# A longer clear between gathers, and every group transposed by itself, in a pairwise-interaction kernel

## The reference

```
e = stack([tbl_f[ids[:, f]] for f in range(32)], axis=1)     # 1024 x 32 x 64
p, q = e[:, ROW], e[:, COL]                                  # the 496 pairs of fields
kp = einsum('bpj,ipj->bpi', p, kernel)                       # kernel 64 x 496 x 64
z = sum(kp * q, axis=-1)                                     # 1024 x 496
h = concatenate([z, dense_ctx], axis=1)                      # 1024 x 512
h = relu(h @ W_top1 + b_top1);  h = relu(h @ W_top2 + b_top2);  y = h @ W_top3
```

## Time and profile before

| | |
|---|---|
| median of 3 runs | 626.92 us (626.18 to 627.76) |
| profiled execution | 622.16 us, span of its instructions 620.2 us |
| granted TensorE clock, mean | 0.884 |
| TensorE busy | 502.4 us (81%) |
| VectorE busy | 305.6 us (49%) |
| GpSimd busy | 273.9 us (44%) |
| ScalarE busy | 67.4 us (11%) |
| DMA, mean | 38 GB/s |

### The profile page before, as it was taken

How to read it: one execution, slowest core, us unless ns; L and a number is a source line. 1 busy time by engine, 2 the same in 40 slices (tenths; PEclk the granted TensorE clock), 3 DMA queues, 4 the chain that set the end, 5 groups by cost and what they waited for, 6 DMA issues and landing times.

```text
span 620.2 us, 10322 instructions
## 1 busy us (share of the span) xinstructions
PE 502.4 (81%) x4290; PEld 309.4 (50%) x4290; DVE 305.6 (49%) x324; ACT 67.4 (11%) x130; POOL 273.9 (44%) x492
## 2 busy tenths in 40 slices
PE   1764444589999786678898768699889999999998
PEld 0432200356666454446565435466566666766443
DVE  3611200166776364337455436467377788787000
ACT  0001000011111021011001001011001211100112
POOL 5888887555557676352727445555700000000000
PEclk9975655599999998798978879899989999999999
DMA  5521212033331111010101011010100030000000
GB/s 154 179 71 23 58 23 61 18 90 90 104 109 43 31 24 26 13 25 9 22 16 23 15 23 28 17 22 17 22 12 1 14 110 10 2 10 2 0 0 0
DMA packets 15318, 23.56 MB, mean 38 GB/s; under 512 B 5506, under 2 KB 7810, under 8 KB 15145
## 3 DMA queue, kind: packets, MB, share of 16 engines
q1 hardware_dynamic: 6884, 14.14, 7.8%
q0 software_dynamic: 7808, 8.01, 6.5%
q10 hardware_dynamic: 580, 0.76, 0.4%
HBM read 20.79 MB, written 0.00 MB: 34 GB/s over the span
## 4 chain that ended last, share of the span: by engine, by line
PE 67%; another core or an unknown queue 13%; issue 10%; DVE 7%; DMA 2%; ACT 0%; SPq 0%; DVEq 0%
PE kp L539 37%; PE z_ps L556 19%; DVE prod L485 6%; PE kp L577 4%; PE tr_ps L523 3%; PE kp L583 2%; PE tr_ps L515 2%; DMA k_sb<-in_tbl 2%; DVE prod L495 1%; PE kp L590 0%; ACT pair L397 0%; ACT prod L441 0%; DVEq L484 0%; SPq L334 0%
## 5 line engine op out<-in xcount | busy, mean ns | idle before, releaser
L485 DVE TENSOR_TENSOR prod<-kp,pair 128x1024 f32<-128x1024 f32 x224 | 261.4, 1218 | 239.0 <-PE kp L539 137.7
L539 PE MATMUL kp<-pair,k_sb 64*128 64x256 f32 x1984 | 286.7, 420 | 63.8 <-issue 32.4
L377 POOL DMA_INDIRECT raw<-in_tbl,ids_sb x244 | 232.8, 954 | 174.8 <-PE tr_ps L523 99.9
L539 PEld LDWEIGHTS kp<-pair,k_sb 64*128 64x128 f32 x1984 | 202.8, 203 | 138.8 <-issue 69.5
L556 PE MATMUL z_ps<-prod,ones_sel 128*32 128x256 f32 x1984 | 141.5, 389 | 24.2 <-issue 22.5
L556 PEld LDWEIGHTS z_ps<-prod,ones_sel 128*32 128x32 f32 x1984 | 65.0, 111 | 94.5 <-issue 57.3
L397 ACT ACTIVATE pair<-tr_ps 128x512 f32<-128x512 f32 (+1 forms) x40 | 20.5, 512 | 351.5 <-PE tr_ps L523 249.4
L381 POOL MEMSET rest<- 128x64 f32 x244 | 40.9, 168 | 0.4
L495 DVE TENSOR_TENSOR prod<-kp,pair 128x512 f32<-128x512 f32 x48 | 30.2, 683 | 8.9 <-issue 6.6
L523 PE MATMUL tr_ps<-ident,raw 128*128 128x128 f32 x122 | 23.8, 309 | 11.4 <-issue 10.8
L515 PE MATMUL tr_ps<-prod,k_sb 125*64 125x256 f32 x96 | 16.6, 521 | 15.7 <-DMA k_sb<-in_tbl 13.4
(11 more groups left out here) (10 smaller groups left out, 9.0 us busy)
## 6 DMA issues: line engine op xcount, KB each, us to landing
k_sb<-in_kd SPq DMA_DIRECT2D x15, 512.0 KB, 3.7
raw<-in_tbl,ids_sb POOLq DMA_INDIRECT x244
pair<-pair SPq DMA_DIRECT2D x32, 64.0 KB
k_sb<-in_tbl SPq DMA_DIRECT2D x6, 250.0 KB
k_sb<-in_w SPq DMA_DIRECT2D x1, 1024.0 KB, 5.0
hot_ids_sb<-in_hot_ids SPq DMA_DIRECT2D x3, 250.0 KB
z_sb<-in_dense ACTq DMA_DIRECT2D x1, 512.0 KB
k_sb<-in_w SPq DMA_DIRECT2D x1, 512.0 KB, 5.7
```

Source lines behind the costliest of these rows:

```text
L377: nc.gpsimd.indirect_dma_start(raw[:, r % RAW_RING, i, n, :], None, tables[f], bass.IndirectOffsetOnAxis(ap=ids_sb[:, 2 * b + i, f:f + 1], ...
L485: nc.vector.tensor_tensor(prod[:, u % PROD_RING, :, :].rearrange("p q (i n) -> p (q i) n", i=UNIT_SLOTS), kp[u % KP_RING][:, :, :].rearran ...
L539: last = nc.tensor.matmul(kp[u % KP_RING][:, q, i * WIDTH:(i + 1) * WIDTH], k_sb[rows, x, :], pair[rows, group_place(st, owner // 2), :], ...
```

## The change

Two constants and the list of places. The clear behind each gather covers 192 columns, not 64 (the scratch tile grows with it). In stages 1 to 3 an event is one group, as in stage 0, so there are 64 events, and the list says where each stands.

```
-REST = 64
+REST = 192

-STAGES = (1, 2, 2, 2)
+STAGES = (1, 1, 1, 1)

-TRANSPOSE_AT = [0, 0, 0, 1, 2, 4, 7, 10, 13, 17, 23, 25, 31, 36, 41, 47, 52, 57, 64, 69, 75, 85, 93, 98, 109, 114,
-                123, 128, 137, 144, 155, 160, 171, 176, 185, 190, 199, 206, 217, 222]
+TRANSPOSE_AT = [0, 0, 0, 1, 2, 4, 7, 10, 13, 17, 23, 25, 31, 36, 41, 47, 52, 57, 61, 63, 64, 66, 69, 72, 75, 79, 85,
+                87, 93, 98, 103, 109, 114, 119, 123, 125, 126, 128, 131, 134, 137, 141, 147, 149, 155, 160, 165,
+                171, 176, 181, 185, 187, 188, 190, 193, 196, 199, 203, 209, 211, 217, 222, 227, 233]
```

## The result

The changed kernel takes 560.19 us (559.72 to 560.39, four runs) against 627.34 for the kernel before beside it: a ratio of 0.8914 (0.8864 to 0.8964), 10.9% faster. The forecast was 24%. The time lies in the range with rivals 1 and 3 (450 to 600 us), not in the forecast's own (455 to 510 us), and the size of the gain does not fit.

A forecast was written before the change was run, and what follows sets the result against it. TensorE sets the pace, but gathers 1.39 us apart delay its signals. Unit 2 at 39.6, 371.5 for 246 units and a 50.4 tail give 461.5 us; with overhead 467, plus 10 makes 477 us, own range 455 to 510.

The forecast's parts named there:

- Rival 1: Only short runs help, spacing does not: the first 80 gathers still hold TensorE back, 550 to 600 us; chance 0.22.
- Rival 3: Cure in part: a load of 1.43 in each 1.53 us delays each signal 1.4 us; 510 to 540 us; chance 0.08.
- a service that each gather needs and that takes about 1.43 us: In runs of gathers 1.39 us apart, this unnamed need builds up a backlog, and TensorE's signals stand behind it.
- My own test: TensorE at half speed before 120 us, lumps 1.5 us apart: no service of 1.43 us exists, rival 1 or 2 holds.
- rival 2: A continuous GpSimd hurts at whatever spacing, and the longer clear is paid on each gather: 661 us, slower; chance 0.16.
- The two rows that "fitted": First eleven gather intervals average 1.45 us, signal at once; recovery took about 4 us after 80 gathers, 1.1 after eight.
- The sum: Whole kernel with signals in time: span 461.5 us, 467 us as median of runs, plus 10 us for imperfections: 477 us.
- 246 units x 1.51 = 371.5 us: TensorE's stretch from unit 2 to the last unit's products, at 1.51 us a unit with signals in time.
- The clear: Behind each gather on GpSimd: 0.14 us more, a gather each 1.53 us, 34 us more in all.
- GpSimd's supply: Gathers end at 378 us, beside TensorE with some 0 to 10 us of slack, costing nothing or a few us.
- The single transposes: In stages 1 to 3 GpSimd is released for four gathers, not eight; ScalarE's 4 us more is hidden.
- the complete cure: Signals in time throughout the kernel: likeliest time 477 us, chance 0.50.

The follow-up runs named there:

- e7: Kernel before, with GpSimd clears in place of all gathers but the first four, clear of 64 columns kept: 448.78 us, ratio 0.7106.
- e14: Kernel before, with a plain copy of the table's first 128 rows in place of each gather, clear of 64 columns kept: 450.24 us, ratio 0.7395.
- e12: Changed kernel with a clear of 288 columns in place of 192, a gather each 1.575 us: 480.96 us, ratio 0.7624.
- e3: Changed kernel with a clear of 320 columns in place of 192, a gather each 1.60 us: 482.21 us, ratio 0.7677.
- e5: Changed kernel with a clear of 256 columns in place of 192, a gather each 1.55 us: 523.82 us, ratio 0.8272.
- e15: Changed kernel with a clear of 448 columns in place of 192, a gather each 1.71 us: 507.67 us, ratio 0.8338.

## Why the prediction was wrong in size

**The step that failed** is "a service that each gather needs and that takes about 1.43 us". From it followed that any spacing over 1.44 us would leave nothing late. At 1.49 us 85 us were late, at 1.55 us 71, and only from 1.575 to 1.60 us did it all but end (37 and 11). I had taken the distance of TensorE's lumps for the time of a service. They follow the gathers: 1.39 gave 1.43 and 1.46, 1.49 gave 1.50. My own test for that stood in the prediction, and it went against me; but the rivals 1 or 2 that were to hold in that case do not hold either. The two rows that "fitted" carried less than I put on them. The first eleven intervals of 1.45 us end at 20.83 us, and TensorE's first products start at 24.6 us. Of the two recoveries only the one of 4 us was worked out (80 x 0.04 = 3.2 us); the same sum gives 8 x 0.04 = 0.3 us for the other, and 1.1 us were measured.

**The sum was right once its condition held.** It gave 477 us with the signals in time throughout; the kernels for which that nearly holds took 481 and 482 us. That it is so near is luck in part: in e7 and e14, where nothing is late, the 246 units take 362 us, 1.47 us each for the 1.51 of the sum, and the whole 449 and 450 us. What e12 and e3 take over that is the signals that are still late and the waits for gathers. The terms in the changed kernel: unit 2 starts at 35.3 us (33 to 39.6 was said), the tail is 50.4 us, as said. The term that failed is 246 units x 1.51 = 371.5 us; it took 507.5 - 35.3 = 472 us, 101 more. Late signals come to 85 us, 5 of them at unit 0; the rest, by argument and not by a run, is a lower clock (0.89 and 0.85 in the first two stretches shown), TensorE's own slowness beside the gathers, and what follows a late signal.

**The clear** cost 0.106 us more and not 0.14: 0.83 ns a column, and 1.49 us a gather for the 1.53 I took. The Trainium skill (GPSIMD Engine Reference, section 3.1), whose 1.03 cycles at 1.2 GHz made 0.11 us and 1.50, was nearer than my two rows; e5, e12, e3 and e15 (0.327, 0.354, 0.381, 0.488 us for 256 to 448 columns) agree with it too (0.83 ns a column for 0.86). A 1-column constant at the start of a program was a poor lower point. It did not matter for the time.

**GpSimd's supply**: the last gather goes out at 400.4 us, not 378, as TensorE was late and held the ring (29.0 us of waits). That supply and demand run side by side was right, and it shows in e3 and bounds e15 (15.9 and 37.0 us of TensorE waiting for gathers).

**The single transposes** did what was said of them where runs became short; what I missed is that the longer clear takes back the pauses that they make. The prediction had this under rival 2, as its price of 0.14 us a gather with an event each 5.9 us. That rival as a whole (a continuous GpSimd hurts at any spacing) is refuted by e3: GpSimd without a pause, and TensorE with 1026 records in 120 us.

**The rivals.** Rival 3, "in part", was the nearest by its mechanism, with 0.08, and said 510 to 540 us: it took one lump of 1.4 us for each signal, and what came is about 5 us at twelve units, and little at most others. Rival 1 covers 560 by number, but its picture is wrong: unit 10 started at 48.6 us, not at 132. I gave half the chance to the complete cure on one reading of two distances; a cure in part, for which the trace of before could give no price, deserved more.

**Of the signs listed**: gathers 1.5 us apart with hardly a pause, right to 172 us (behind it there are 22 pauses, 32 us in all, to 400 us); unit 10 before 60 us, right; TensorE over 90% busy from 40 to 120 us, wrong (77%); unnamed waits of VectorE and ScalarE under 20 us, wrong (92.0 and 134.9).

What stays open is the mechanism below the indirect form: what it shares with TensorE or its semaphores, and whether the engine or only its signals are held first. The runs show that halving bytes or rows changes next to nothing, that the same number of packets by plain copies does no harm, and that the mean spacing of the gathers decides. That TensorE's own rate has a part is read from where the late signals stand (behind the sums), not shown by a run; no record shows the thing itself.

## What to carry to other kernels

When an engine waits for something that the profile can't name, and the waits end as soon as another engine pauses, vary that engine's rate and nothing else: a sweep of the clear from 192 to 320 columns (0.8914, 0.8272, 0.7624, 0.7677) told more than any reading of the stall itself. A distance between records in a disturbed stretch is not the capacity of what disturbs it; it may be the disturber's own period. Idle time put on purpose on an engine that is not the bound can be the cheapest gain of all, up to the point at which its supply becomes the bound; here that was 1.575 to 1.60 us a gather, and 24% of the time.

## What the runs showed of the hardware that was not expected

- Indirect DMAs issued by GpSimd each 1.39 us hold back TensorE's semaphore signals, mostly by 3 to 12 us as VectorE sees them; ScalarE got one 19.3 us late. With 1.60 us from one to the next at most 1.0 us is left (e3, behind unit 0), and it is not there with plain DMAs of the same packets each 0.99 us (450.24 us for the whole kernel).
- An indirect DMA of 64 rows takes GpSimd 0.914 us, one of 128 rows 0.951, and a plain copy of 128 rows 0.536.
- A clear on GpSimd takes 0.168, 0.274, 0.381 and 0.488 us for 64, 192, 320 and 448 columns: 0.83 ns a column. Clears alone, each set of three in 1.00 us, hold nobody up (448.78 us for the whole kernel).
